# The product delta*u*B moves from a PSUM bank to SBUF, and its bank joins the ring of TensorE's outputs

## The chip, the cores and the metric

One core of one Trainium2 chip runs the whole program in one launch. The metric is the device time of that launch in microseconds. The kernel before took 9698.47 us (median of three runs, 9694.0 to 9716.83).

## The reference

Sixteen images of 64 channels and 64x64 pixels go through two 3x3 convolutions with a leaky ReLU, then through a selective state space layer over the 4096 pixels (128 inner channels, 16 states each), then through two attentions (over channels and over positions) with a residual. The part around the change is the recurrence of the state space layer:

```
def step(h, inp):
    d_t, u_t, b_t, c_t = inp
    h = jnp.exp(d_t[..., None] * A) * h + (d_t * u_t)[..., None] * b_t[:, None, :]
    y = jnp.einsum('bdn,bn->bd', h, c_t)
    return (h, y)
```

The attention over positions needs a softmax over 4096 x 4096 scores for each image:

```
energy_s = jnp.einsum('bcn,bcm->bnm', q, k)
attn_s = jax.nn.softmax(energy_s, axis=-1)
out_s = jnp.einsum('bcm,bnm->bcn', v, attn_s).reshape(b, c, h, w)
```

## The kernel before

A first stage does the convolutions of all images, two at a time. The second stage is a software pipeline over images: while image j goes through the recurrence, the attention of the images before it runs on TensorE. A step of this pipeline has 128 **ticks** (TICKS). An image's 128 channels x 16 states are 16 groups of 128 lanes, and its 4096 pixels are 8 slices of 512, so a tick is one group in one slice, and sixteen ticks are one slice. All instructions of a step stand in an order written out by the program, tick by tick, on each engine; semaphores tie the engines together.

In one tick T the engines do this:

- **ScalarE (ACT)**: two exponentials of attention scores (L948, `pr`), the decay `dA` = exp(delta*A) of tick T+1 (L954, which waits for the scan of T-1), a one-column copy of the last state of the scan of T-1 (L959, `carry`), a ReLU of score differences into `gains` (L894), and evacuations of small matmuls (L939).
- **VectorE (DVE)**: the product `DBU` = (delta*u)*B of tick T (L1081), the scan (L1089, `hst`), in most ticks one operation on the preparation of the next slice or the finish of the last (L1074 to L1151), and the running maximum of the scores (L1034, which reads a bank and `gains`).
- **GpSimd (POOL)**: `hst` times C for tick T-1 (L1189), after the scan and the carry of T-1. Once in a slice it also makes `ysb` (L1195) and `usp` (L1201).
- **TensorE (PE)**: two score tiles (L829 and L831), the values of the tick before (L840), one or two pairs of score tiles for the maxima (L777, the uses "dif" and "max"), the row sums every second tick (L853), the sum over states every fourth tick (L864), and a few small matmuls (xin, z, dt, BC, out, xv, en and others).

The eight PSUM banks are divided: banks 0 to 3 are a **ring** (RB). Every use (a score tile, a dif, a max, a small matmul) takes the next bank in the order of the program, and may start when the use that had this bank before it has been read. The other four banks have one owner each: the product DBU, the values' accumulator ACC, the row sums DEN and the states' sum YPS.

```
def take_bank(e):
    if number[e] >= RING:
        taken(pe, sched.uses[number[e] - RING])
    return bank_of(e)
```

A score tile is read by ScalarE (semaphore p_full), a max by VectorE (dve_took), a dif and most small uses by ScalarE (act_took).

Of the kernel before, what the change touches and what calls it, by code (L numbers as in the profile page):

```python
# [23 lines left out]
P = 128  # L24
# [10 lines left out]
CHUNK = 512  # L35
# [21 lines left out]
HRING = 8  # L57
BATCH = 4
SLOTS = 4
# [38 lines left out]
def group_of(T):  # L98

    k = T % GROUPS  # L100
    return k % BLOCKS * GPB + k // BLOCKS
# [128 lines left out]

SIGNAL_OF = {"PV": "pv", "SUM": "den", "Y": "y_mm"}
DVE_USES = ("max", "turn", "mix", "res", "en")
RING = 4


def build(nc, x, w1, b1, w2, b2, w_in, cw, cb, w_dt_t, w_dt, dt_b, w_bc, a_log, skip, w_out,
          w_out_t, w_cam_t, w_qk_t, w_v, w_bn1_t, w_bn2_t, consts, out):
    seq_d = nc.dram_tensor("seq_d", [IMAGES, CH, L], F32, kind="Internal").ap()
    x1_d = nc.dram_tensor("x1_d", [IMAGES, CH, L], F32, kind="Internal").ap()
    parts_d = nc.dram_tensor("parts_d", [IMAGES, 2, 3, QDIM, L], BF16, kind="Internal").ap()  # L240
    kx_d = nc.dram_tensor("kx_d", [IMAGES, 2, QDIM, L], BF16, kind="Internal").ap()
    bc_d = nc.dram_tensor("bc_d", [2, 2 * D_STATE, CHUNK], F32, kind="Internal").ap()
    spread_d = nc.dram_tensor("spread_d", [2, P, 2, CHUNK], F32, kind="Internal").ap()
    vt_d = nc.dram_tensor("vt_d", [IMAGES, P, KT, CH], F32, kind="Internal").ap()

    with ExitStack() as top:
        banks = [top.enter_context(nc.psum_tensor(f"bank{i}", [P, 512], F32)) for i in range(8)]
        convolutions(nc, banks, x, w1, b1, w2, b2, seq_d)
        pipeline(nc, banks, seq_d, (x1_d, parts_d, kx_d, vt_d, spread_d, bc_d), w_in, cw, cb, w_dt_t,
                 w_dt, dt_b, w_bc, a_log, skip, w_out, w_out_t, w_cam_t, w_qk_t, w_v, w_bn1_t,  # L250
                 w_bn2_t, consts, out)
# [141 lines left out]
def pipeline(nc, banks, seq_d, scratch, w_in, cw, cb, w_dt_t, w_dt, dt_b, w_bc, a_log, skip,  # L393
             w_out, w_out_t, w_cam_t, w_qk_t, w_v, w_bn1_t, w_bn2_t, consts, out):
    x1_d, parts_d, kx_d, vt_d, spread_d, bc_d = scratch
    RB, (DBU, ACC, DEN, YPS) = banks[0:RING], banks[RING:]
    AUX = RB[0]
    with ExitStack() as ctx:
        def sb(name, shape, dt=F32):
            return ctx.enter_context(nc.sbuf_tensor(name, shape, dt))  # L400
# [24 lines left out]
        bbc = sb("bbc", [P, 2, CHUNK])  # L425
# [6 lines left out]
        usp = sb("usp", [P, CHUNK])  # L432
        lanes = sb("lanes", [P, SLOTS, 2, CHUNK])
        dA = sb("dA", [P, 2, CHUNK])
        hst = sb("hst", [P, HRING, CHUNK])
        carry = sb("carry", [P, GROUPS])
        ysb = sb("ysb", [P, CHUNK])
# [97 lines left out]
        def step(j, i):  # L535
# [9 lines left out]
            def wait(eng, name, event, times=1):  # L545

                value = sched.counts.get(name, {}).get(event)
                if value is not None:
                    eng.wait_ge(S[name], value * times)  # L549
# [5 lines left out]
            def bank_of(e):  # L555
                return RB[number[e] % RING]

# [5 lines left out]
            def taken(eng, e):  # L563

                if e in sched.freed:
                    eng.wait_ge(S[sched.freed[e][0]], sched.freed[e][1])


            for T in range(sched.first, sched.last):
                sl, r = T // GROUPS, T % GROUPS  # L570
# [54 lines left out]
            with nc.Block() as block:  # L625
# [132 lines left out]
                def _(pe):  # L758
# [5 lines that stand above are left out]
# [252 lines left out]
                def _(dve):  # L1016
# [50 lines left out]
                    for T in range(first, last):  # L1067
                        sl, r = T // GROUPS, T % GROUPS
# [7 lines left out]
                        if sched.scans(T):  # L1076
                            wait(dve, f"lanes{T % SLOTS}", T, 16)
                            if r == 0:
                                wait(dve, "ld_b", sl, 16)
                            wait(dve, "scan", T - 1)  # L1080
                            nc.vector.tensor_tensor(DBU[:], lanes[:, T % SLOTS, 1, :], bbc[:, sl % 2, :],  # L1081
                                                    ALU.mult).then_inc(
                                S["dbu_in"], 1)
                        if sched.scans(T):
                            g = group_of(T)
                            wait(dve, "dbu_in", T)
                            wait(dve, "da_in", T)
                            wait(dve, "y_mm", ((T - HRING) // BATCH,))
                            nc.vector.tensor_tensor_scan(  # L1089
                                hst[:, T % HRING, :], dA[:, T % 2, :], DBU[:],  # L1090
                                carry[:, g:g + 1] if sl else 0.0, ALU.mult, ALU.add).then_inc(S["scan"], 1)
                        c = sl + 1
                        if sched.prepares(c):
# [157 lines left out]
```

## Time and profile before

| | |
|---|---|
| runs | 9694.0 to 9716.83 us, median 9698.47 us |
| the profiled execution's own time | 9699.92 us |
| its span, from first to last instruction | 9698.1 us |
| mean granted TensorE clock, as a share of full | 0.954 |
| TensorE, VectorE, ScalarE, GpSimd busy | 8341.3, 7451.8, 6341.1, 3263.7 us |

The convolutions end at about 820 us. The first scan begins at 840.2 us and the last at 9136.4 us, so the ticks with a scan fill some 8296 us, 2048 of them at 4.05 us each. After that only attention is left. A busy share is a mean over all of this; what sets the time is read from the waits and from the order of operations in a tick.

### The profile page before, as it was taken

How to read it: one execution, taken by the hardware profiler on the slowest of the kernel's cores; microseconds unless marked ns; L12 is line 12 of the kernel's file. 1: busy time of each engine (PE TensorE's matmuls, PEld its weight loads, DVE VectorE, ACT ScalarE, POOL GpSimd, SP SyncE). 2: the span in 40 equal slices, each digit the busy share in tenths (PEclk: the TensorE clock that was granted, in tenths of full speed). 3: DMA queues.
4: the chain of work that ended last, by engine and by line, in shares of the span. 5: the costliest groups of instructions: out<-in, count | busy, mean ns of one | idle time of the engine just before them, and what ended most of it. 6: DMA issues, size and time to landing. Idle time of an engine off the chain costs nothing. (4 is left out here: it accounts for less than half of the span.)

```text
span 9698.1 us, 136670 instructions
## 1 busy us (share of the span) xinstructions
PE 8341.3 (86%) x38979; PEld 2211.9 (23%) x39622; DVE 7451.8 (77%) x11112; ACT 6341.1 (65%) x12445; POOL 3263.7 (34%) x2315
## 2 busy tenths in 40 slices
PE   8884349898989898998989898989989898989999
PEld 2221012222222222222222222222222222222222
DVE  1115988888888888888888888888888888988632
ACT  1113457776767777776767777777777776777654
POOL 0003544333333333333333333333434333433200
PEclk9996569999999999999999999999999999999999
DMA  6455876666667676667667676767666666667400
GB/s 91 81 92 139 207 191 168 169 171 168 174 161 181 156 184 162 179 168 174 169 168 176 160 179 163 180 163 182 170 171 171 167 170 170 175 162 179 117 21 8
DMA packets 799817, 1512.11 MB, mean 156 GB/s; under 512 B 347752, under 2 KB 381232, under 8 KB 799024
## 3 DMA queue, kind: packets, MB, share of 16 engines
q1 hardware_dynamic: 795952, 1502.62, 63.3%
q8 instruction: 316, 5.18, 0.3%
q14 instruction: 477, 3.91, 0.2%
q10 hardware_dynamic: 3072, 0.40, 0.0%
HBM read 1309.36 MB, written 176.16 MB: 153 GB/s over the span
## 5 line engine op out<-in xcount | busy, mean ns | idle before, releaser
L1189 POOL TENSOR_TENSOR hst<-hst,cbc 128x512 f32<-128x512 f32 x2048 | 2849.0, 1392 | 5005.8 <-ACT carry L959 4223.5
L948 ACT ACTIVATE pr<-bank 128x512 f32<-128x512 f32 x4096 | 2230.9, 596 | 1181.2 <-PE bank L831 1167.2
L1089 DVE TENSOR_TENSOR_SCAN hst<-dA,carry,bank 128x512 f32<-128x512 f32 x1792 | 2293.9, 1280 | 67.0 <-ACT dA L954 2.9
L840 PE MATMUL bank<-pr,vt 128*64 128x512 f32 x8192 | 2245.2, 627 | 0.0
L1034 DVE CUSTOM_DVE_ANT_0 gains<-bank,gains 128x512 f32<-128x512 f32 x2048 | 1391.0, 687 | 894.3 <-ACT gains L894 867.9
L1081 DVE TENSOR_TENSOR bank<-lanes,bbc 128x512 f32<-128x512 f32 x2048 | 1699.2, 830 | 191.5 <-issue 119.5
L829 PE MATMUL bank<-s1q,s1k 128*128 128x512 bf16 x3453 | 1336.1, 387 | 550.9 <-DMA t2q<-nm 168.4
L954 ACT ACTIVATE dA<-lanes,small 128x512 f32<-128x512 f32 x2048 | 1486.4, 726 | 278.2 <-DMA lanes<-spread_d 179.5
L831 PE MATMUL bank<-t2q,t2k 128*128 128x512 bf16 x4096 | 1568.7, 383 | 87.7 <-issue 43.5
L894 ACT ACTIVATE gains<-bank 128x512 f32<-128x512 f32 x2048 | 1225.1, 601 | 501.8 <-PE bank L777 469.1
L777 PE MATMUL bank<-s1kx,s1q 128*128 128x512 bf16 x4096 | 1298.5, 388 | 188.4 <-DVE mxp L1034 137.2
L853 PE MATMUL bank<-pr,ones 128*32 128x512 f32 x8192 | 1093.4, 606 | 0.0
L829 PEld LDWEIGHTS bank<-s1q,s1k 128*128 128x128 bf16 x4096 | 398.5, 97 | 1988.7 <-issue 911.0
L777 PEld LDWEIGHTS bank<-s1kx,s1q 128*128 128x128 bf16 x4096 | 263.4, 97 | 1969.5 <-issue 1310.4
L864 PE MATMUL bank<-hst,cst 128*32 128x512 f32 x4096 | 571.2, 631 | 89.3 <-POOL hst L1189 89.3
L840 PEld LDWEIGHTS bank<-pr,vt 128*64 128x64 f32 x8192 | 408.4, 136 | 881.9 <-issue 866.7
L365 ACT ACTIVATE biased<-bank,bias 128x512 f32<-128x512 f32 x128 | 88.0, 687 | 640.7 <-PE bank L352 640.7
L831 PEld LDWEIGHTS bank<-t2q,t2k 128*128 128x128 bf16 x4096 | 403.9, 99 | 344.8 <-issue 108.4
L352 PE MATMUL bank<-xpad,w1tap 128*64 128x512 f32 x1536 | 349.1, 618 | 110.9 <-DMA xpad<-in_x 110.9
L959 ACT COPY carry<-hst 128x1 f32<-128x1 f32 x1792 | 339.5, 189 | 0.0
L376 DVE SCALAR_TENSOR_TENSOR ypad<-biased 64x512 f32<-64x512 f32 x64 | 43.8, 685 | 376.9 <-ACT biased L365 376.9
L352 PE MATMUL bank<-ypad,w2tap 128*64 128x512 f32 x1536 | 330.9, 592 | 0.0
(110 smaller groups left out, 6398.8 us busy)
## 6 DMA issues: line engine op xcount, KB each, us to landing
lanes<-spread_d SPq DMA_DIRECT2D x2048, 512.0 KB, 5.0
seqt<-seq_d SPq DMA_DIRECT2D x256, 128.0 KB, 4.5
spread_d<-dsp SPq DMA_DIRECT2D x128, 256.0 KB, 2.0
spread_d<-usp SPq DMA_DIRECT2D x128, 256.0 KB, 2.0
bbc<-bc_d SPq DMA_DIRECT2D x128, 256.0 KB, 3.4
cbc<-bc_d SPq DMA_DIRECT2D x128, 256.0 KB, 3.9
xpad<-in_x SPq DMA_DIRECT2D x64, 256.0 KB, 6.6
ypad<-ypad SPq DMA_DIRECT2D x128, 128.0 KB, 2.8
```

The costliest lines, as they stand in the source:

```text
L777: mm = nc.tensor.matmul(bank[:].rearrange("p (c n) -> p c n", n=HALF), s1q[:, q % 2, nt * P:(nt + 1) * P], keys[:, 2 * mc:2 * (mc + 1), 1 ...
L829: nc.tensor.matmul(bank[:], s1k[:, t * P:(t + 1) * P], s1q[:, q % 2, cols], start=True, stop=False)
L831: nc.tensor.matmul(bank[:], t2k[:, t * P:(t + 1) * P], t2q[:, q % 2, cols], start=False, stop=True).then_inc(S["ring_full"], 1)
L840: mm = nc.tensor.matmul(ACC[CH * h:CH * (h + 1), :], vt[:, t, :], pr[:, T % PRING, h, :], start=t == 0, stop=t == KT - 1)
L853: mm = nc.tensor.matmul(DEN[o:o + 32, :], ones[:], pr[:, (2 * p + par) % PRING, h, :], start=t == 1, stop=t == KT - 1, tile_position=(0, o))
L894: nc.scalar.activation(gains[:, k % 2, :], bank_of(e)[:], ACT.Relu).then_inc(S["act_took"], 1)
L948: nc.scalar.activation(pr[:, T % PRING, h, :], bank_of(("S", T, h))[:], ACT.Exp).then_inc(S["p_full"], 1)
L954: nc.scalar.activation(dA[:, (T + 1) % 2, :], lanes[:, (T + 1) % SLOTS, 0, :], ACT.Exp, scale=amat[:, g:g + 1]).then_inc(S["da_in"], 1)
L1034: nc.vector.tensor_tensor_reduce(out=gains[:, k % 2, :], in0=bank[:], in1=gains[:, k % 2, :], scale=1.0, scalar=LOWEST, op0=ALU.add, op1=A ...
L1081: nc.vector.tensor_tensor(DBU[:], lanes[:, T % SLOTS, 1, :], bbc[:, sl % 2, :], ALU.mult).then_inc(S["dbu_in"], 1)
L1089: nc.vector.tensor_tensor_scan(hst[:, T % HRING, :], dA[:, T % 2, :], DBU[:], carry[:, g:g + 1] if sl else 0.0, ALU.mult, ALU.add).then_in ...
L1189: nc.gpsimd.tensor_tensor(h, h, cbc[:, (T - 1) // GROUPS % 2, :], ALU.mult).then_inc(S["hc_in"], 1)
```

## The change

The product gets an SBUF tile of its own. The ring becomes banks 0 to 4, and the other three owners keep banks 5, 6 and 7. The product's inputs were and are in SBUF. The scan had one input in SBUF (`dA`) and one in PSUM (the product); now both are in SBUF. No instruction is added, removed or moved on any engine, and the semaphores of product and scan stay.

```
 DVE_USES = ("max", "turn", "mix", "res", "en")
-RING = 4
+RING = 5
...
-    RB, (DBU, ACC, DEN, YPS) = banks[0:RING], banks[RING:]
+    RB, (ACC, DEN, YPS) = banks[0:RING], banks[RING:]
...
         dA = sb("dA", [P, 2, CHUNK])
+        dbu = sb("dbu", [P, CHUNK])
...
-                            nc.vector.tensor_tensor(DBU[:], lanes[:, T % SLOTS, 1, :], bbc[:, sl % 2, :],
+                            nc.vector.tensor_tensor(dbu[:], lanes[:, T % SLOTS, 1, :], bbc[:, sl % 2, :],
...
-                                hst[:, T % HRING, :], dA[:, T % 2, :], DBU[:],
+                                hst[:, T % HRING, :], dA[:, T % 2, :], dbu[:],
```

The ring's length changes which use each matmul waits for. On TensorE, in the early part of a step, this is one whole tick (two score tiles, the values, a dif and a max, the row sums) in the kernel before; in brackets stand the semaphores waited for:

```order
L829 MATMUL bank3<-s1q,s1k 128x512 [waits p_full]
L831 MATMUL bank3<-t2q,t2k 128x512
L829 MATMUL bank0<-s1q,s1k 128x512 [waits act_took]
L831 MATMUL bank0<-t2q,t2k 128x512
L840 MATMUL bank5<-pr,vt 64x512 [waits p_full]
L840 MATMUL bank5<-pr,vt 64x512
L777 MATMUL bank1<-s1kx,s1q 128x512 [waits dve_took]
L777 MATMUL bank2<-s1kx,s1q 128x512 [waits act_took]
```

and the same tick in the changed kernel:

```order
L830 MATMUL bank2<-s1q,s1k 128x512 [waits p_full]
L832 MATMUL bank2<-t2q,t2k 128x512
L830 MATMUL bank3<-s1q,s1k 128x512 [waits p_full]
L832 MATMUL bank3<-t2q,t2k 128x512
L841 MATMUL bank5<-pr,vt 64x512 [waits p_full]
L841 MATMUL bank5<-pr,vt 64x512
L778 MATMUL bank4<-s1kx,s1q 128x512 [waits act_took]
L778 MATMUL bank0<-s1kx,s1q 128x512 [waits dve_took]
```

Every row stands where it stood. Each use waits for the use five before it instead of four before it: here VectorE's reading of a maximum is asked for by the second tile of the pair and no longer by the first.

## Rows read from the trace of the kernel before

**Rows 1.** The page: each engine's busy time in us, its share of the span, instructions.

```profile
PE 8341.3 (86%) x38979; PEld 2211.9 (23%) x39622; DVE 7451.8 (77%) x11112; ACT 6341.1 (65%) x12445; POOL 3263.7 (34%) x2315
```

**Rows 2.** Busy time by stretch: length, PE, PEld, DVE, ACT, POOL, PEclk, DMA share, GB/s.

```profile
4500.00:9000.00 4500.00, 4050.30 (x19140) 1051.95 (x19489) 3878.68 (x5820) 3317.25 (x6573) 1729.29 (x1230) 0.98 0.68 171
```

**Rows 3.** Waits: engine, line, what it waited for, us in total, times, longest.

```profile
DVE gains L1034 <- ACT gains L894: 867.9, 789, 10.4
...
DVE accs L1157 <- PE bank L840: 207.4, 64, 44.7
...
PE bank L777 <- DVE mxp L1034: 137.2, 177, 3.4
...
PE bank L829 <- ACT pr L948: 131.3, 116, 1.6
...
PE bank L864 <- POOL hst L1189: 89.3, 17, 11.8
PE bank L829 <- DVE mxp L1034: 83.8, 191, 0.9
```

**Rows 4.** Sources of the scan and the maximum: durations min/median/max, first and last start.

```profile
L1089 DVE TENSOR_TENSOR_SCAN hst<-dA,carry,bank x1792: 1278/1280/1283, 886.1 to 9136.4; 128x512 f32<-128x512 f32 x200
L1089 DVE TENSOR_TENSOR_SCAN hst<-dA,bank x256: 1219/1220/1222, 840.2 to 8686.4; 128x512 f32<-128x512 f32 x128
L1034 DVE CUSTOM_DVE_ANT_0 gains<-bank,gains x2048: 664/691/693, 1316.7 to 9589.5; 128x512 f32<-128x512 f32 x187
```

**Rows 5.** The same of operations with two SBUF inputs, on DVE and POOL.

```profile
L1081 DVE TENSOR_TENSOR bank<-lanes,bbc x2048: 679/695/1808, 839.3 to 9135.7; 128x512 f32<-128x512 f32 x187
L1105 DVE SCALAR_TENSOR_TENSOR cacc<-xin,small,cacc x384: 723/726/1655, 817.3 to 9031.7; 128x512 f32<-128x512 f32 x192
L1189 POOL TENSOR_TENSOR hst<-hst,cbc x2048: 1252/1276/2046, 844.9 to 9146.0; 128x512 f32<-128x512 f32 x187
```

**Rows 6.** Timeline (start us, length us), product delayed by GpSimd.

```profile
4199.30 1.27 POOL L1189 TENSOR_TENSOR hst<-hst,cbc 128x512 f32<-128x512 f32 x1 [3.23 <-ACT carry L959]
4199.90 1.22 DVE L1081 TENSOR_TENSOR bank<-lanes,bbc 128x512 f32<-128x512 f32 x1
```

**Rows 7.** Timeline, GpSimd begins within L1105, and the product follows.

```profile
4330.41 0.73 DVE L1105 SCALAR_TENSOR_TENSOR cacc<-xin,small,cacc 128x512 f32<-128x512 f32 x1
4330.58 1.70 POOL L1189 TENSOR_TENSOR hst<-hst,cbc 128x512 f32<-128x512 f32 x1 [0.27 <-DVE hst L1089]
4331.18 1.66 DVE L1081 TENSOR_TENSOR bank<-lanes,bbc 128x512 f32<-128x512 f32 x1
```

**Rows 8.** Timeline, first and last of the 520 scans that begin under a GpSimd operation.

```profile
851.79 1.33 POOL L1189 TENSOR_TENSOR hst<-hst,cbc 128x512 f32<-128x512 f32 x1 [0.99 <-ACT carry L959]
852.04 1.22 DVE L1089 TENSOR_TENSOR_SCAN hst<-dA,bank 128x512 f32<-128x512 f32 x1
...
9095.10 1.65 POOL L1195 TENSOR_TENSOR ysb<-ysb,zs 128x512 f32<-128x512 f32 x1 [0.97 <-DVE ysb L1074]
9095.66 1.28 DVE L1089 TENSOR_TENSOR_SCAN hst<-dA,carry,bank 128x512 f32<-128x512 f32 x1
```

**Rows 9.** Timeline, first and last of the 560 scans within which GpSimd begins.

```profile
846.76 1.22 DVE L1089 TENSOR_TENSOR_SCAN hst<-dA,bank 128x512 f32<-128x512 f32 x1
846.95 1.26 POOL L1189 TENSOR_TENSOR hst<-hst,cbc 128x512 f32<-128x512 f32 x1 [0.78 <-ACT carry L959]
...
9049.06 1.28 DVE L1089 TENSOR_TENSOR_SCAN hst<-dA,carry,bank 128x512 f32<-128x512 f32 x1
9050.27 1.27 POOL L1189 TENSOR_TENSOR hst<-hst,cbc 128x512 f32<-128x512 f32 x1 [1.80 <-ACT carry L959]
```

**Rows 10.** Sources of two like sums, one with an input in PSUM, one without.

```profile
L1058 DVE TENSOR_TENSOR accs<-accs,bank x64: 681/681/689, 1607.5 to 9689.4; 128x512 f32<-128x512 f32 x64
L1166 DVE TENSOR_TENSOR accs<-accs,dens x64: 691/692/693, 1596.2 to 9688.6; 128x512 f32<-128x512 f32 x64
```

**Rows 11.** The page's costliest groups: busy us, mean ns, idle before and releaser.

```profile
L1081 DVE TENSOR_TENSOR bank<-lanes,bbc 128x512 f32<-128x512 f32 x2048 | 1699.2, 830 | 191.5 <-issue 119.5
...
L954 ACT ACTIVATE dA<-lanes,small 128x512 f32<-128x512 f32 x2048 | 1486.4, 726 | 278.2 <-DMA lanes<-spread_d 179.5
```

## The prediction

> **What bounds the kernel now.** I read the page first. TensorE is busy for 86% of the span, VectorE for 77%, ScalarE for 65% [rows 1]. The mean hides the stages, so I took the busy time of a stretch in which every tick has its scan: there TensorE is at 4050 of 4500 us (90%), VectorE at 3879 (86%), ScalarE at 3317 (74%) and GpSimd at 1729 (38%) [rows 2]. No engine is full. Two stand close together and hold each other up. The chain that ended last is of no use here, since the page follows it only through the attention at the end. So the table of waits is the next view [rows 3]. VectorE's largest wait is the maximum's, for `gains` from ScalarE: 868 us in 789 pieces. TensorE waits for banks of the ring: 137 us at L777 and 84 us at L829 for VectorE's maxima, and 131 us at L829 for ScalarE's exponentials, together 352 us. The last view is the timeline of VectorE and GpSimd alone, because the change alters what VectorE reads.
>
> **What the two engines do to each other.** The scan's length is the same in all 1792 cases, 1278 to 1283 ns, and so is the maximum's, 664 to 693 ns: each reads one operand from PSUM and one tensor from SBUF [rows 4]. Operations of VectorE that read two tensors from SBUF are different: the product has a median of 695 ns and reaches 1808, L1105 has 726 and reaches 1655, and GpSimd's product has 1276 and reaches 2046 [rows 5]. The timeline shows why. A product that began at 4199.90, while GpSimd worked until 4200.57, took 1.22 us instead of 0.695: 0.525 us more, where GpSimd had 0.67 left [rows 6]. At 4331.18 GpSimd had 1.10 us left (4330.58 + 1.70) and the product took 1.66, so 0.965 more [rows 7]. So such an operation is lengthened by what is left of GpSimd's, less about 0.135 us. The same rows tell who wins when both want to go: GpSimd's began inside L1105 (4330.41 to 4331.14), was stretched from 1.26 to 1.70, so stood still until L1105 had ended, and then the product waited, not GpSimd [rows 7]. The scan did not mind: one that began at 852.04 with 1.08 us of GpSimd's left (851.79 + 1.33) took its 1.22, and one at 9095.66 with 1.09 us left took its 1.28 [rows 8].
>
> The Trainium skill says this in "SBUF — State Buffer", section "Who interferes with whom": a VectorE instruction with at most one SBUF input doesn't contend with GpSimd, one with two does, and whichever comes second waits for the whole of the other. The trace agrees for every operation named above; no row of this kernel shows a scan with two SBUF inputs.
>
> **The change part by part.**
>
> *The product's output.* It goes to SBUF instead of PSUM, at the same two inputs: L1105, which writes SBUF and does two operations an element, has 726 ns against its 695 [rows 5], and the sum L1166 has 692 [rows 10]. From both sides that is 2048 x (-30 to +30 ns), so -60 to +60 us of VectorE; I take 0.
>
> *The scan's own length.* No row has both inputs in SBUF. The nearest pair are the sums L1058 (one input in PSUM, 681 ns) and L1166 (both in SBUF, 691 ns) [rows 10]: 2048 x 0.01 = 20 us more; the other bound is as much less. I take 0. The Trainium skill's page "VectorE: DVE Perf Modes", section "The TRN2 errata", gives a PSUM source 120 cycles of fixed cost and an SBUF source 58. By it the scan would gain 62 cycles at 0.96 GHz, 65 ns, an estimate of 132 us over 2048 scans. The pair L1058 and L1166 shows no such gain, with the other sign if any.
>
> *The scan held up by GpSimd, directly.* In the timeline, 520 of the 2048 scans begin while a GpSimd operation is under way, with 1.10 us of it left in the mean (1.08 for the first, 1.09 for the last) [rows 8]. Less 0.135 us each that is 520 x 0.965 = 502 us. The bounds: 0, if a scan is not held at all, and one collision in every tick (below).
>
> *GpSimd held up by the scan, and what it holds up then.* Another 560 scans have GpSimd beginning inside them, 0.57 us before their end in the mean (1.03 for the first: 846.95 against 846.76 + 1.22; 0.07 for the last) [rows 9]. It would stand until the scan has ended and then run 1.26 us. GpSimd's own lateness is covered: it is busy 38% of the time [rows 2], and TensorE waited for it 89 us in all [rows 3]. But it then wins against VectorE's next operation with two SBUF inputs. Going through the 560 cases, 440 have such an operation within those 1.26 us, and the added wait is 0.41 us in the mean over all 560: 232 us. Together VectorE gets 502 + 232 = 734 us more work.
>
> *What hides it.* The cover is VectorE's idle time before the maxima, 868 us. The wait for the last values at L1157 (207 us) [rows 3] is no cover: it hangs on TensorE's whole order. Added work of 734 us x 4500 / 8296 is 398 us in the stretch of rows 2, and brings VectorE from 3879 to 4277 of 4500 us, 95%. An engine that is tied to two others in every tick doesn't reach that: TensorE, the fullest now, stands at 90%. If VectorE reaches 91 to 93%, the stretch takes 4277/0.93 = 4599 to 4277/0.91 = 4700 us, 2.2 to 4.4% more, over 8296 us 183 to 369 us. A second way: half of the 734 us falls before an idle piece and is hidden, half lands, 367 us. What is late next is ScalarE's `dA` and carry, which wait for the scan, and TensorE's matmul into the bank whose maximum has not been read.
>
> *The fifth bank.* It can at most take away TensorE's 352 us of bank waits [rows 3]. Waiting for a use one place earlier moves a wait by a score tile or a dif, some 0.4 to 0.8 us of TensorE, where the waits are 0.44 us (84/191) to 1.13 us (131/116) each. That would remove about half, 176 us, if VectorE were free to follow. With VectorE fuller than TensorE, the waits for its maxima (221 of the 352) only move. I take 90 us, from 0 to 352.
>
> The sum: 367 - 90 = 277 us, and the middle of the utilisation estimate (276) agrees. Against the profiled execution's 9699.9 us that is 9977 us; the median of the runs is 1.4 us lower, which changes nothing. I predict **9980 us**. What a measurement of this kernel can't tell from no change is 0.3%, 29 us, so between 9669 and 9728.
>
> **The rivals.**
>
> 1. *The collisions lock into step (slower still).* Once VectorE is the last in every tick, ScalarE waits for the scan, then does `dA` (0.73 us) [rows 11] and the short copy of the carry, and GpSimd begins some 1 us after the scan's end: in the next product or just before it, so it delays product or scan in every tick. For it speaks that this pattern is there already where VectorE has no idle time [rows 7]. If 1500 of 2048 ticks paid 0.965 us, that is 1448 us, of which the product pays 1699 - 2048 x 0.695 = 276 us today [rows 11]. Of the other 1172 us 367 are hidden and 90 won back: 10,410 us.
> 2. *The scan is not held (faster).* Its rows are unlike any other operation's: it takes 2.5 ns an element where the others take 1.3 [rows 4, 5], and a reader at half the pace may leave room for GpSimd. Then only the ring counts: 176 us less, 9520 us. Against it: every kind of two-input operation in the rows is held [rows 5].
> 3. *The scan is held, but the fifth bank outweighs it (faster).* That needs nearly all of the 734 us to fall into the 868 us of idle time. The deeper ring helps in that, since it lets TensorE and ScalarE go on while VectorE is late. With 600 hidden and 200 won: 9634 us. It decides in its favour if less than a quarter of the delays lands. Against it: within a slice, ticks in which VectorE is busy all the time come in runs, and there nothing is hidden.
> 4. *The two cancel (no change).* 9700 us.
>
> **How the numbers follow.** My forecast (a net loss of 0.3% to some 4.5%) has 0.62, rival 1 0.13, rival 2 0.10, rival 3 0.08, rival 4 0.07. Faster is 2 and 3, 0.18, same 0.07, slower 0.75. The range leaves out rival 2 and part of rival 1: 9630 to 10,350 us. The forecast's own range is 9740 to 10,200.
>
> **What the changed profile would show.** The scan's minimum stays at 1278 ns (within 20) and its maximum goes beyond 2200; its mean is 1.5 us or more in place of 1.27. GpSimd's product has more and longer stretched cases. VectorE's busy time rises by 600 to 1000 us, its wait before L1034 falls by half, and TensorE's waits for ScalarE's exponentials fall while those for maxima don't. If the scan's durations stay in one narrow band, rival 2 holds. If they spread but VectorE's idle time falls by as much as its work rises, it is rival 3. The prediction would be wrong above all if the order of collisions changed: the 520 and 560 are counted in the phase that the engines keep now.

## The result, and the profile of the changed kernel

The changed kernel took **10,442.8 us** (median of five runs, 10,435.6 to 10,447.8), 1.0763 times the kernel before (95% interval 1.0747 to 1.0778). It is 744 us slower; 282 us were forecast, and the range ended at 10,350.

Each engine's busy time in the changed kernel, from the page of its profile, against [rows 1]:

```profile
span 10433.8 us, 136668 instructions
PE 8593.5 (82%) x38979; PEld 2246.6 (22%) x39622; DVE 8305.3 (80%) x11112; ACT 6374.9 (61%) x12445; POOL 3463.8 (33%) x2315
```

VectorE is 8305.3 - 7451.8 = 853 us busier with the same 11112 instructions. Its scan, product and maximum by source line (durations min/median/max), against [rows 4, 5]:

```profile
L1090 DVE TENSOR_TENSOR_SCAN hst<-dA,carry,dbu x1792: 1282/1284/2374, 893.1 to 9875.5; 128x512 f32<-128x512 f32 x200
L1090 DVE TENSOR_TENSOR_SCAN hst<-dA,dbu x256: 1224/1225/2286, 840.3 to 9392.8; 128x512 f32<-128x512 f32 x128
L1082 DVE TENSOR_TENSOR dbu<-lanes,bbc x2048: 671/690/1800, 839.4 to 9874.2; 128x512 f32<-128x512 f32 x187
L1035 DVE CUSTOM_DVE_ANT_0 gains<-bank,gains x2048: 658/691/694, 1375.8 to 10325.2; 128x512 f32<-128x512 f32 x187
```

Undisturbed, the scan takes what it took before (1284 against 1280 ns), but it is not always undisturbed: its longest case is 2374 ns, where it was 1283. The maximum, still with one operand in PSUM, stays in its band. One collision in the timeline (start, length), and what follows it:

```profile
5022.78 1.27 POOL L1190 TENSOR_TENSOR hst<-hst,cbc 128x512 f32<-128x512 f32 x1 [0.85 <-ACT carry L960]
...
5022.86 2.27 DVE L1090 TENSOR_TENSOR_SCAN hst<-dA,carry,dbu 128x512 f32<-128x512 f32 x1
5025.06 0.72 DVE L1106 SCALAR_TENSOR_TENSOR cacc<-xin,small,cacc 128x512 f32<-128x512 f32 x1
5025.23 0.72 ACT L955 ACTIVATE dA<-lanes,small 128x512 f32<-128x512 f32 x1 [0.55 <-DVE hst L1090]
```

GpSimd had 1.19 us left when the scan began (5022.78 + 1.27 - 5022.86), and the scan took 0.99 us longer than its 1.28; in the kernel before, the same arrangement left the scan alone [rows 8]. ScalarE's next decay then waited for the scan. The waits, against [rows 3]:

```profile
DVE gains L1035 <- ACT gains L895: 797.3, 622, 10.5
...
ACT dA L955 <- DVE hst L1090: 454.1, 399, 4.1
...
PE bank L778 <- DVE mxp L1035: 451.9, 290, 3.7
...
PE bank L830 <- DVE mxp L1035: 242.9, 141, 2.5
```

The first line matters most. VectorE has 853 us more to do, the program got 744 us longer, and the idle time that was to hide half of the added work only went from 868 to 797 us. Of these, 271 us (before) and 267 us (changed) lie behind the last scan, where no scan and no product of the recurrence is left to be delayed; in the part with scans the idle time before the maxima went from 597 to 531 us. TensorE's waits for VectorE's maxima went from 221 to 695 us, although the ring has a bank more.

### The profile page after: what moved, and what is told of

It reads as the page before. It is cut to its first block and busy times, and to the rows that moved or that the text cites. A ratio compares the mean times of both kernels' runs of the same rounds, so it can differ in the third digit from the quotient of the medians.

```text
span 10433.8 us, 136668 instructions
## 1 busy us (share of the span) xinstructions
PE 8593.5 (82%) x38979; PEld 2246.6 (22%) x39622; DVE 8305.3 (80%) x11112; ACT 6374.9 (61%) x12445; POOL 3463.8 (33%) x2315
## 5 line engine op out<-in xcount | busy, mean ns | idle before, releaser
L1190 POOL TENSOR_TENSOR hst<-hst,cbc 128x512 f32<-128x512 f32 x2048 | 3045.1, 1488 | 5517.1 <-ACT carry L960 4747.3
L1090 DVE TENSOR_TENSOR_SCAN hst<-dA,carry,dbu 128x512 f32<-128x512 f32 x1792 | 2658.6, 1484 | 66.6 <-ACT dA L955 1.9
L841 PE MATMUL bank<-pr,vt 128*64 128x512 f32 x8192 | 2334.1, 650 | 0.0
L1082 DVE TENSOR_TENSOR dbu<-lanes,bbc 128x512 f32<-128x512 f32 x2048 | 1906.4, 931 | 170.8 <-issue 118.5
L830 PE MATMUL bank<-s1q,s1k 128*128 128x512 bf16 x3453 | 1378.3, 399 | 645.8 <-DVE mxp L1035 242.9
L832 PE MATMUL bank<-t2q,t2k 128*128 128x512 bf16 x4096 | 1620.3, 396 | 96.7 <-issue 46.8
L865 PE MATMUL bank<-hst,cst 128*32 128x512 f32 x4096 | 616.0, 677 | 98.4 <-POOL hst L1190 98.4
L832 PEld LDWEIGHTS bank<-t2q,t2k 128*128 128x128 bf16 x4096 | 410.7, 100 | 393.4 <-issue 152.3
L1106 DVE SCALAR_TENSOR_TENSOR cacc<-xin,small,cacc 128x512 f32<-128x512 f32 x384 | 405.1, 1055 | 19.6 <-ACT cacc L982 18.8
L1090 DVE TENSOR_TENSOR_SCAN hst<-dA,dbu 128x512 f32<-128x512 f32 x256 | 374.2, 1462 | 9.1
```

What stands on the lines that cost most here:

```text
L830: nc.tensor.matmul(bank[:], s1k[:, t * P:(t + 1) * P], s1q[:, q % 2, cols], start=True, stop=False)
L832: nc.tensor.matmul(bank[:], t2k[:, t * P:(t + 1) * P], t2q[:, q % 2, cols], start=False, stop=True).then_inc(S["ring_full"], 1)
L841: mm = nc.tensor.matmul(ACC[CH * h:CH * (h + 1), :], vt[:, t, :], pr[:, T % PRING, h, :], start=t == 0, stop=t == KT - 1)
L1082: nc.vector.tensor_tensor(dbu[:], lanes[:, T % SLOTS, 1, :], bbc[:, sl % 2, :], ALU.mult).then_inc(S["dbu_in"], 1)
L1090: nc.vector.tensor_tensor_scan(hst[:, T % HRING, :], dA[:, T % 2, :], dbu[:], carry[:, g:g + 1] if sl else 0.0, ALU.mult, ALU.add).then_in ...
L1190: nc.gpsimd.tensor_tensor(h, h, cbc[:, (T - 1) // GROUPS % 2, :], ALU.mult).then_inc(S["hc_in"], 1)
```

## The experiments

Each ratio is to the kernel before, run on the same chip alongside, with its 95% interval in brackets. Times longer or shorter in us are differences of the two medians, which can differ by some us from what the ratio gives. "Busier" is against the profile of the kernel before. In the code cuts, `...` marks what is left out.

**The ring stays at four, the product is in SBUF (ring4_sbuf).**

```
-RING = 5
+RING = 4
...
-    RB, (ACC, DEN, YPS) = banks[0:RING], banks[RING:]
+    RB, (SPARE, ACC, DEN, YPS) = banks[0:RING], banks[RING:]
```

> The product in SBUF as in the changed kernel, but the ring stays at four banks and the fifth stays unused. Theory (the scan with two SBUF inputs and GpSimd's operations hold each other up, and the ring gives little): the scan's durations spread to 2.2 us and more as in the changed kernel, VectorE is again some 850 us busier than before, and the time is 10,440 us, or up to 176 us more if the fifth bank was worth what the prediction's upper term says. Rival (the longer ring is what costs, because TensorE and ScalarE run ahead in another phase): 9,700 to 10,000 us.

10,489 us, ratio 1.0801 (1.0781 to 1.0820), 787 us longer. The scan has a mean of 1465 ns and VectorE is 746 us busier, about 100 us less than expected. So the whole loss comes from the product's place, and none from the longer ring. The fifth bank is worth 0.4%, some 40 us.

**The same load on VectorE without added collisions (extra_vector_work).**

```
+EXTRA = 240
...
                             wait(dve, "dbu_in", T)
+                            nc.vector.tensor_copy(junk[:, 0:EXTRA], DBU[:, 0:EXTRA])
```

> The kernel before with one more VectorE operation in each tick, between product and scan: a copy of 240 columns from the product's PSUM bank into a tile that nobody reads. It has one input in PSUM and so shouldn't meet GpSimd. At some 0.41 us it adds 840 us to VectorE, as much as the change did (853 us). Theory (VectorE's added time lands nearly whole, its idle time before the maxima is no cover, whatever it is that lengthens VectorE): 10,350 to 10,500 us. Rival (half is covered, as the prediction had it, and the change lost the rest by what comes with a collision: late carries, GpSimd's own lateness): 10,050 to 10,150 us.

10,393 us, ratio 1.0706 (1.0682 to 1.0730). The copy reads PSUM and has one duration, 407 to 410 ns, whatever GpSimd does:

```profile
L1089 DVE COPY junk<-bank x2048: 407/407/410, 840.9 to 9824.7; 128x240 f32<-128x240 f32 x187
```

VectorE is 800 us busier and the program 691 us longer, 86% of it. So VectorE's added time reaches the program's time even where no collision causes it.

**GpSimd's product on 8 of 512 columns, in both kernels (before_short_pool, after_short_pool).** These two leave out 504 of 512 columns of the multiplication by C, so their sums y are not the reference's.

```
-                            nc.gpsimd.tensor_tensor(h, h, cbc[:, (T - 1) // GROUPS % 2, :],
+                            nc.gpsimd.tensor_tensor(h[:, 0:8], h[:, 0:8], cbc[:, (T - 1) // GROUPS % 2, 0:8],
...
```

> The kernel before, but GpSimd's product hst times C works on 8 of its 512 columns (the output is wrong in y; all waits stay). It takes away most collisions. Theory: the product's spread is gone, VectorE is 400 to 500 us less busy, and nearly all of that shows in the time: 9,250 to 9,350 us. Rival (VectorE's idle time covered it): 9,500 to 9,700 us.

> The changed kernel with GpSimd's product on 8 of 512 columns, so the fifth bank and the product in SBUF are seen without their collisions. Theory: the scan's durations are one narrow band at 1283 ns again, the whole loss of 743 us is gone, and against the kernel before with the same short GpSimd product it is faster by the fifth bank's worth, 0 to 176 us. Rival (the scan or the product are slower from SBUF by themselves, or the longer ring costs): slower than that kernel by 100 us and more.

9,532 us (0.9820, 0.9802 to 0.9838) and 9,486 us (0.9774, 0.9756 to 0.9793). With GpSimd's product nearly gone the changed kernel is no longer slower but 46 us faster than its counterpart. That is the fifth bank, 0.4 to 0.5% as above, or a little more: VectorE is still 65 us busier than in the counterpart. The second expectation's narrow band didn't come: 89 scans were still held, up to 2336 ns, all by GpSimd's two operations of a slice (`ysb` and `usp`), which kept their 512 columns. The first expectation missed by 200 us: VectorE was 486 us less busy, but only 170 us of it showed. Taking this work off VectorE brought a third of it, adding 800 us cost nearly all.

**Half the scans (half_decays_psum).** Ring of four; the decays of the even ticks lie in the spare bank.

```
-                            nc.scalar.activation(dA[:, (T + 1) % 2, :], lanes ...
+                            nc.scalar.activation(SPARE[:] if (T + 1) % 2 == 0 else dA[:, 1, :], lanes ...
...
-                                hst[:, T % HRING, :], dA[:, T % 2, :], dbu[:],
+                                hst[:, T % HRING, :], SPARE[:] if T % 2 == 0 else dA[:, 1, :], dbu[:],
```

> Ring of four, product in SBUF; the spare bank holds the decays of the even ticks, so only the scans of odd ticks have two inputs in SBUF. Theory: even scans are never longer than 1290 ns, odd ones spread as in the kernel with the ring of four and all scans exposed (10,489 us); the loss against the kernel before is about half of 787 us or somewhat less, since half of the spread goes and what is added first costs less: 9,950 to 10,100 us. Rival (the place of the product, not the number of SBUF inputs, is what costs): still some 10,490 us.

9,980 us, ratio 1.0273 (1.0240 to 1.0305). The scans of one kernel, the even ones first:

```profile
L1090 DVE TENSOR_TENSOR_SCAN hst<-bank,carry,dbu x896: 1282/1283/1285, 890.4 to 9414.5; 128x512 f32<-128x512 f32 x180
L1090 DVE TENSOR_TENSOR_SCAN hst<-dA,carry,dbu x896: 1282/1284/2248, 892.5 to 9417.7; 128x512 f32<-128x512 f32 x180
```

The product is in SBUF for both. Only where the other tensor is in SBUF too do the durations spread. And the even scans were not spared by chance: 374 of them, those of the first slices included, began while a GpSimd operation was under way, and none took longer than 1285 ns. For the scan it is the number of SBUF inputs that decides, not the product's place. The loss is a third of that with all scans exposed.

**The ring from the other side (ring_of_three).** The kernel before with `RING = 3` and a spare bank.

> The kernel before with a ring of three banks, the fourth unused. It shows the worth of a bank from the other side. Theory (banks have little worth at four and more because VectorE sets the pace; the fifth was worth 46 us): the fourth is worth more, 150 to 500 us, so 9,850 to 10,200 us. Rival (bank waits only stand for other waits): within 60 us of 9,700 us.

10,131 us, ratio 1.0432 (1.0413 to 1.0452). The fourth bank is worth 4%, the fifth some 0.4 to 0.5%.

**Half the extra load (extra_work_half).** The copy of 240 columns only if `T % 2`.

> The extra VectorE copy of 240 columns in odd ticks only, so 400 us instead of 800 us. Theory (the idle time before the maxima covers nothing: VectorE's added time lands at once): 280 to 350 us more, some 10,000 us. Rival (the cover exists but is small, and is used up first): 100 to 250 us more, and the second half costs the rest of the 691 us.

10,005 us, ratio 1.0297 (1.0275 to 1.0319), 285 us longer. VectorE is 508 us busier, 417 by the copy and most of the rest by the product, whose mean went from 830 to 877 ns. So 56% landed, against 86% of 800 us: some cover exists, and is used up.

**The same load in lumps (extra_work_lumps).** Two copies of together 1.0 us if `T % 5 in (0, 3)`.

> The kernel before with the same extra VectorE work as 240 columns in every tick (some 820 us), but in lumps: two copies of together 1.0 us in two ticks of five, about as long and as frequent as the collisions of the changed kernel. Theory (a delay costs by its length, not only by its sum, since banks hide short ones): slower than the even one (10,393 us) by 50 to 150 us, some 10,480 us. Rival (only the sum counts): within 40 us of 10,393 us.

10,161 us, ratio 1.0484 (1.0449 to 1.0519): VectorE is 739 us busier, the program 446 us longer. Neither expectation held: lumps cost less, not more. A single delay's length of 1 us is not what makes collisions dear.

**Where the lumps fall (extra_work_full_ticks, extra_work_idle_ticks).** In the trace of the kernel before, VectorE's waits (all that last over 0.15 us, mean of a tick) sit in certain ticks of each slice: 2.1 us in tick 0, 2.0 in tick 15, 1.2 in tick 9, 0.9 in tick 1, 0.3 in ticks 11 and 13, and at most 0.03 in ticks 3, 5, 6, 8, 10 and 12. The same 768 lumps went once on full ticks, once on idle ones; `r` is the tick's number in its slice.

```
+EXTRA = 160
...
+                            if r in (3, 5, 6, 8, 10, 12):      # extra_work_full_ticks
+                            if r in (0, 1, 9, 11, 13, 15):     # extra_work_idle_ticks
+                                nc.vector.tensor_copy(junk[:], DBU[:])
+                                nc.vector.tensor_copy(junk2[:, 0:EXTRA], DBU[:, 0:EXTRA])
```

> The kernel before with the extra lumps (two copies of together 1.0 us) on six of sixteen ticks, 3, 5, 6, 8, 10 and 12 of each slice, in which VectorE has no idle time in the kernel before; 768 lumps, some 775 us. Theory (what counts is whether VectorE has idle time in the very tick, and collisions fall where it has none): 650 to 775 us slower, 10,350 to 10,480 us. Rival (idle time is no slack, place doesn't matter): as the lumps on two ticks of five, 440 to 520 us slower.

> The same lumps on ticks 0, 1, 9, 11, 13 and 15 of each slice, where VectorE idles for 0.33 to 2.2 us in the kernel before. Theory: much of it hidden, 0 to 350 us slower, 9,700 to 10,050 us. Rival: 440 to 520 us slower, as the lumps on two ticks of five.

10,385 us (1.0695, 1.0657 to 1.0732) and 9,824 us (1.0115, 1.0078 to 1.0151). The added copies take the same time to a microsecond; the waits tell the two kernels apart:

```profile
L1091 DVE COPY junk<-bank 128x512 f32<-128x512 f32 x768 | 530.9, 691 | 26.3
L1092 DVE COPY junk<-bank 128x160 f32<-128x160 f32 x768 | 241.6, 315 | 0.0
...
DVE gains L1037 <- ACT gains L897: 795.9, 643, 10.2
PE bank L780 <- DVE mxp L1037: 439.4, 326, 3.8
```

on full ticks, and on idle ticks

```profile
L1091 DVE COPY junk<-bank 128x512 f32<-128x512 f32 x768 | 531.0, 691 | 26.4
L1092 DVE COPY junk<-bank 128x160 f32<-128x160 f32 x768 | 241.6, 315 | 0.0
...
DVE gains L1037 <- ACT gains L897: 526.9, 475, 10.2
PE bank L780 <- DVE mxp L1037: 187.7, 201, 3.3
```

772 us of copies cost 670 us on full ticks and 110 us on idle ones. A part of the difference is that VectorE's other operations were held up less than before: its busy time grew by 660 and by 569 us, not by 772. This net growth landed whole on full ticks, and to a fifth on idle ones. On full ticks VectorE's idle time hardly falls (868 to 796 us) and TensorE's wait at the maximum's bank triples from 137 us; on idle ticks the idle time takes much of the work (527 us left). The pattern of the full ticks is that of the changed kernel, 797 us and 452 us.

**Does TensorE's clock pay a part (filler_matmuls).** Its granted clock has a mean of 0.925 in the changed kernel and 0.954 before.

```
+                        if kind == "max":
+                            nc.tensor.matmul(SPARE[:] ..., s1q[...], keys[...], start=True, stop=True)
                         bank = take_bank(e)
```

> The kernel with the product in SBUF and a ring of four (10,489 us), with one more score matmul of 512 columns into the unused bank ahead of each use for a maximum, where TensorE waits for VectorE; nobody reads it. It tells whether TensorE's granted clock (mean 0.929 there, 0.954 in the kernel before) is part of the loss. Theory (it is: TensorE idles while VectorE is held up, the clock falls, and everything behind TensorE is later still): the clock rises to 0.94 or more and the time falls by 50 to 200 us, to 10,290 to 10,440 us. Rival (the clock only follows, VectorE sets the pace): the clock rises, and the time stays within 40 us or grows by up to 200 us of TensorE's added work.

10,667 us, ratio 1.0994 (1.0962 to 1.1026), 178 us longer than without the filler. But the clock hardly rose, 0.932 against 0.929, so neither theory was put to the test. Whether the clock pays a part stays open.

**GpSimd's place in the tick (pool_under_scan, own_tile_under_scan, own_tile_at_once).** Three versions of the kernel before. The first makes GpSimd wait until the product of the next tick is done, so that it runs beside the scan:

```
                             wait(pool, "carried", T - 1)
+                            wait(pool, "dbu_in", T)
```

> The kernel before with one more wait: GpSimd's product for tick T-1 also waits until VectorE's product of tick T is done, so it begins with the scan of T, which has one input in PSUM and doesn't meet it; scan (1.28 us) and GpSimd's operation (1.26 us) are equally long. Theory: collisions go, VectorE's busy time falls by 300 to 450 us (the product's 276 us of stretch and more), and as removing 486 us of it by a short GpSimd product brought 166 us, this brings 90 to 160 us: 9,540 to 9,610 us, faster than both kernels. Rival (GpSimd's lateness makes TensorE wait for the states' sums, or VectorE's next operation with two inputs is hit instead): 9,700 us or more.

9,689 us, ratio 0.9968 (0.9957 to 0.9978). The sign is as expected, but it brought 31 us where 90 to 160 were expected: GpSimd still waited 3454 us for ScalarE's copy of the carry and so came late in many ticks; the product's mean fell only from 830 to 770 ns. The second version takes the carry out of the way: GpSimd writes to a tile of its own with eight slots, and TensorE reads that.

```
+        hc = sb("hc", [P, HRING, CHUNK])
...
-                                                  hst[:, (BLOCKS * b + j) % HRING, :],
+                                                  hc[:, (BLOCKS * b + j) % HRING, :],
...
-                            wait(dve, "y_mm", ((T - HRING) // BATCH,))
+                            wait(dve, "hc_in", T - HRING)
+                            wait(dve, "carried", T - HRING)
...
-                            wait(pool, "carried", T - 1)
+                            wait(pool, "dbu_in", T)
+                            wait(pool, "y_mm", ((T - 1 - HRING) // BATCH,))
-                            nc.gpsimd.tensor_tensor(h, h, cbc[...], ALU.mult)
+                            nc.gpsimd.tensor_tensor(hc[:, (T - 1) % HRING, :], h, cbc[...], ALU.mult)
```

> The kernel before, with GpSimd writing hst times C to a tile of its own (eight slots) instead of over hst, so that it no longer waits for ScalarE's copy of the carry, and with the wait for VectorE's product of the next tick as in the kernel with GpSimd under the scan. GpSimd should then begin with the scan in nearly every tick. Theory: the product's stretch (276 us before, 159 us with that wait alone) falls under 60 us, VectorE is 250 to 400 us less busy, and the time falls by 90 to 160 us: 9,560 to 9,620 us. Rival (two-input operations behind the scan are hit instead, or late sums stop TensorE): 9,690 us and more.

**9,531 us**, ratio 0.9821 (0.9792 to 0.9850): faster than both kernels. Two ticks of its timeline:

```profile
4199.94 0.69 DVE L1082 TENSOR_TENSOR bank<-lanes,bbc 128x512 f32<-128x512 f32 x1
4200.66 1.28 DVE L1091 TENSOR_TENSOR_SCAN hst<-dA,carry,bank 128x512 f32<-128x512 f32 x1
4200.76 1.27 POOL L1192 TENSOR_TENSOR hc<-hst,cbc 128x512 f32<-128x512 f32 x1 [1.90 <-DVE bank L1082]
4201.86 0.72 DVE L1122 SCALAR_TENSOR_TENSOR zs<-em,zs 128x512 f32<-128x512 f32 x1
4202.51 0.68 DVE L1035 CUSTOM_DVE_ANT_0 gains<-bank,gains 128x512 f32<-128x512 f32 x1
4203.11 0.08 DVE L1035 DVE_READ_ACCUMULATOR2_ANT mxp<- 128x1 f32 x1
4203.11 0.69 DVE L1082 TENSOR_TENSOR bank<-lanes,bbc 128x512 f32<-128x512 f32 x1
4203.84 1.28 DVE L1091 TENSOR_TENSOR_SCAN hst<-dA,carry,bank 128x512 f32<-128x512 f32 x1
4203.94 1.27 POOL L1192 TENSOR_TENSOR hc<-hst,cbc 128x512 f32<-128x512 f32 x1 [1.90 <-DVE bank L1082]
```

GpSimd's 1.27 us lie under the scan's 1.28. The product's mean is 700 ns, VectorE is 452 us less busy, and the time equals that with GpSimd's product on 8 columns (9,532 us), so next to nothing of its cost is left. The third version is the same without the wait for the product, and so shows that this wait, and not the tile of its own, brings the gain.

> As that kernel but without the wait for VectorE's product: GpSimd begins as soon as a scan has ended, so under the maximum (0.69 us) and then into the next product (or at once against a two-input operation). Theory (the place of GpSimd's 1.26 us in VectorE's tick decides): more collisions than with the wait, VectorE busier by 300 us and more than there, and the time 100 to 400 us above it. Rival (being early is what counts): equal or faster.

9,744 us, ratio 1.0047 (1.0026 to 1.0068). GpSimd starts when the scan ends and runs into the product, whose mean is 995 ns; VectorE is 241 us busier than in the kernel before. To start earlier is worse.

**The same place in the changed kernel (own_tile_five_banks).** The edit of own_tile_under_scan, made in the changed kernel.

> The changed kernel (product in SBUF, ring of five) with GpSimd's result in a tile of its own and with its wait for VectorE's product, so that it wants to start with the scan, as in the fastest kernel so far (9,531 us). Theory (the scan has two SBUF inputs, so GpSimd stands until it has ended and then holds up VectorE's next two-input operation in nearly every tick): GpSimd's product takes 2.4 us in the mean, VectorE is 900 us and more busier than in the kernel before, 10,300 to 10,900 us. Rival (the fixed place helps here too): below 9,700 us.

10,434 us, ratio 1.0752 (1.0711 to 1.0793). GpSimd's product and the scan in the table of groups (busy us, mean ns):

```profile
L1193 POOL TENSOR_TENSOR hc<-hst,cbc 128x512 f32<-128x512 f32 x2048 | 4580.5, 2237 | 3966.2 <-DVE dbu L1083 3150.8 <-issue 802.4 <-POOLq L263 7.0
L1092 DVE TENSOR_TENSOR_SCAN hst<-dA,carry,dbu 128x512 f32<-128x512 f32 x1792 | 2315.5, 1292 | 65.4 <-ACT carry L961 1.6
```

Now the scan is first and GpSimd stands until it has ended. Its operation takes 2.24 us in the mean and then holds up what VectorE does next; VectorE is 1031 us busier than in the kernel before. With the product in SBUF the longest operation of every tick that leaves GpSimd alone is the maximum with its 0.69 us, about half of what GpSimd's operation needs.

## Why the prediction was wrong

**Right: the mechanism.** VectorE's two-input operations and GpSimd exclude each other, and the scan joined them. That it does was the unproven step, and half_decays_psum shows it inside one kernel. Writing the product to SBUF changed nothing (a median of 690 against 695 ns), nor did the scan's own length (4 ns).

The Trainium skill's rule in "SBUF — State Buffer", section "Who interferes with whom", holds for the scan as it stands: the trace agrees, by 1285 ns at most with one SBUF tensor and up to 2248 with two. The prediction told this rule without its condition: the section exempts an instruction with one SBUF input only outside the modes that use two ports, which it says tensor_scalar, copy and cast can enter. The trace agrees: the tensor_scalar L1127, which takes 0.40 us for 512 columns where a copy of 512 columns from PSUM took 0.69, has one SBUF input and is held all the same (last section). The 62 cycles (65 ns, an estimate) that the Trainium skill's page "VectorE: DVE Perf Modes", section "The TRN2 errata", would have given back are not there: 1284 ns from SBUF, 1280 from PSUM.

**Nearly right: VectorE's added work.** Forecast 734 us, measured 853. The direct part: 454 scans instead of 520 began under a GpSimd operation, with 1.11 us left in the mean, and took 0.92 us longer (what is left less 0.195, not less 0.135): 416 us against 502. The rest fell on other operations, 437 us where 232 were forecast: the product pays 1906 - 1699 = 207 us more, and L1106, L1127, L1137 and L1147 the most of what remains.

**Wrong: "What hides it".** This is the step that failed. It took VectorE's 868 us of idle time before the maxima for a cover and let "half of the 734 us" be hidden, "half lands, 367 us". Of 853 us some 70 were hidden (744 landed, plus about 40 that the fifth bank gave back), and nearly all the rest landed. Two things about the 868 us were in the trace of the kernel before and were not looked at.

First, 271 of them lie behind the last scan, and cannot hide anything. Second, the other 597 us sit in few ticks (a tick counted here from one product to the next). In nine of the sixteen ticks of a slice (2 to 6, 8, 10, 12 and 14) there were 39 us of them in all. In the changed kernel VectorE's operations are lengthened by 889 us more than before (the sum of what each takes beyond the shortest of its kind, where that is over 60 ns), and 732 us of this fell in those nine ticks. The same sum shows that what is hidden in one tick can come back in another: ticks 7 and 9 had 213 us of idle time before their maxima and lost 189 of it, while ticks 11 to 13 had 69 us and gained 159. That place decides the price is shown by 670 against 110 us for the same lumps. Why the collisions fall mostly in the ticks without idle time is open. It is not that an idle piece keeps GpSimd out of VectorE's way: in the changed kernel the operations from one maximum to the next were lengthened by 0.97 us in the mean where the first maximum had waited, and by 0.55 us where it had not. The prediction itself had named the reason for doubt, in its case against rival 3: "ticks in which VectorE is busy all the time come in runs, and there nothing is hidden".

The step's other way, a busy share of 91 to 93%, failed with it: between first and last scan VectorE went from 7163 of 8296 us (86.3%) to 8017 of 9035 (88.7%). That the middle of this way (276 us) agreed with the sum (277 us) was no support either, since the 276 us had no term for the fifth bank and the 277 had. The forecast's upper end doesn't fit its words: 4.5% would be 10,135 us, not 10,200.

**Wrong in size: the fifth bank.** 90 us were forecast, 37 us (with collisions, from the ratios) to 46 us (nearly without) measured.

**Rival 1** named the time better than the forecast (10,410 us), and half by luck. It was right that collisions become more frequent: VectorE's operations that began under a GpSimd operation and took over 60 ns too long went from 759 to 1752, and the ticks with such an operation from 684 to 1307. But it expected 1172 us of added work, where 853 came, and hid 367 us of it, where some 70 were hidden; the two errors nearly cancel. Nor was VectorE the last in every tick: 489 maxima of the part with scans still waited for ScalarE, 655 before.

Still open: why VectorE's 746 us of added work cost 787 us, a little more than their sum, with the ring of four. VectorE's idle time grew there by 55 us, 39 of them before the maxima. TensorE's clock fell from a mean of 0.954 to 0.929, and its matmuls took longer (L832 has a mean of 396 ns in the changed kernel, the same line 383 before); whether the time follows from it was not shown.

## What to carry to other kernels

Before an operand moves between PSUM and SBUF, count the SBUF inputs of every VectorE operation that reads it, and look whether GpSimd works at that time: here a PSUM bank was worth 787 us as the product's place and some 40 us as a fifth output bank. If GpSimd has to read SBUF beside VectorE, tie its start to a VectorE operation with one SBUF input that is as long as its own. And before idle time is counted as cover, ask in which ticks it lies, and whether it lies in the part where the delays fall at all: the same 772 us cost 670 or 110.

## What was not expected of the hardware

When GpSimd's operation waits for one of VectorE's and another of VectorE's stands behind, GpSimd goes first: in the kernel before it did in all 94 cases in which two-input operations of VectorE followed each other and GpSimd began within the first [rows 7]. A waiting operation shows no idle time but a longer duration (GpSimd 2237 ns for 1260), so the busy time of VectorE and GpSimd holds time in which they do nothing; a mean over the instruction's minimum tells how much. Operations of VectorE with a single tensor, in SBUF, are lengthened as well: the tensor_scalar L1127 in the changed kernel, 87 of 128 times by a mean of 1.0 us, and already in the kernel before the small cast L1047 (8x128), 58 of 64 times by 1.06 us, each of the 58 having begun under a GpSimd operation.
